# A mixture-of-experts layer in which the last slots are 11 tiles of two chunks and 7 of one chunk, in place of 18 tiles of two

## The reference

```
x = x + attention(layernorm(x))                       # 8 x 512 x 256, causal
xn = layernorm(x, gamma, beta)
probs = softmax(xn @ gate_w);  w, idx = top_k(probs, 2);  w = w / sum(w)
h = gelu(xn @ w1[e] + b1[e])                          # 256 -> 1024, exact gelu
out = sum over the two experts of w_e * (h @ w2[e] + b2[e])   # 1024 -> 256
x = x + (xn + out)
```

## Time and profile before

| | |
|---|---|
| time, median of 3 runs | 1096.27 us |
| the profiled execution | 1091.03 us |
| its span, first to last instruction | 1089.1 us |
| TensorE busy | 911.5 us (84%) |
| VectorE busy | 731.8 us (67%) |
| ScalarE busy | 596.7 us (55%) |
| GpSimd busy | 471.4 us (43%) |
| mean granted TensorE clock | 0.887 of full |

### The profile page before, as it was taken

The page is one execution under the profiler, slowest core; times in us unless marked ns, Lnnn a source line. Parts: engine busy times, 40 slices in busy tenths (PEclk is TensorE's granted clock), DMA queues, the critical chain, the costliest instruction groups (busy, mean ns, idle before and its releaser), DMA issues.

```text
span 1089.1 us, 21658 instructions
## 1 busy us (share of the span) xinstructions
PE 911.5 (84%) x7052; PEld 598.0 (55%) x7052; DVE 731.8 (67%) x1632; ACT 596.7 (55%) x1085; POOL 471.4 (43%) x536
## 2 busy tenths in 40 slices
PE   4788868775878787888887898879988999999995
PEld 2444423222242323333332787768877898989894
DVE  6353688775648798887883686766756676767663
ACT  2554537563747677766766564444634454545451
POOL 2000003323424565646565557454564555455542
PEclk9898988887678887879785999989999999999998
DMA  9887757764665757575735552232322333332322
GB/s 208 266 287 247 257 191 221 227 160 112 187 205 153 212 158 201 144 212 137 196 86 164 180 114 41 42 84 41 46 42 46 55 46 55 46 55 45 56 45 25
DMA packets 150568, 144.22 MB, mean 132 GB/s; under 512 B 42112, under 2 KB 128896, under 8 KB 150336
## 3 DMA queue, kind: packets, MB, share of 16 engines
q1 hardware_dynamic: 117856, 97.92, 31.4%
q0 software_dynamic: 17024, 20.81, 11.9%
q10 hardware_dynamic: 15584, 24.12, 6.9%
HBM read 88.44 MB, written 54.10 MB: 131 GB/s over the span
## 4 chain that ended last, share of the span: by engine, by line
PE 38%; DMA 17%; issue 11%; DVE 10%; SPq 7%; POOL 7%; ACT 6%; DVEq 2%; ACTq 0%; POOLq 0%
PE banks L729 13%; PE banks L713 13%; DMA qk_parts<-weights 4%; DMA arena<-in_L_ffn_w 4%; SPq L1779 3%; POOL slot_tokens L1556 3%; PE banks L635 2%; PE banks L592 2%; PE banks L647 2%; POOL out L1600 2%; DMA weighed_values<-arena 1%; DVE arena L1160 1%; DMA late_weights<-arena 1%; SPq L1766 1%; PE banks L577 1%
## 5 line engine op out<-in xcount | busy, mean ns | idle before, releaser
L935 ACT ACTIVATE arena<-banks,arena 128x256 f32<-128x256 f32 x312 | 158.9, 561 | 197.9 <-issue 130.3
L729 PE MATMUL banks<-weights,arena 128*128 x1872 | 217.0, 275 | 9.0 <-DVE arena L1419 8.9
L713 PE MATMUL banks<-arena,weights 128*128 128x256 f16 x1872 | 213.1, 274 | 3.9 <-DMA weights<-late_weights 3.0
L1600 POOL DMA_INDIRECT out<-arena x78 | 128.0, 1641 | 202.5 <-DVE arena L1430 101.2
L729 PEld LDWEIGHTS banks<-weights,arena 128*128 128x128 f16 x1872 | 183.8, 99 | 34.6 <-issue 12.1
L713 PEld LDWEIGHTS banks<-arena,weights 128*128 x1872 | 183.7, 98 | 27.2 <-issue 4.9
L592 PE MATMUL banks<-arena 50*128 50x128 f16 (+3 forms) x512 | 125.7, 352 | 36.2 <-ACT arena L862 13.9
L564 PE MATMUL banks<-arena 48*128 48x128 f16 (+3 forms) x512 | 103.2, 345 | 34.8 <-DVE arena L1158 25.9
L1419 DVE SCALAR_TENSOR_TENSOR arena<-arena 128x512 f16<-128x512 f32 x156 | 119.3, 765 | 5.6
L592 PEld LDWEIGHTS banks<-arena 50*128 50x128 f16 x512 | 38.2, 102 | 147.1 <-issue 52.7
L1417 DVE TENSOR_SCALAR arena<-arena 128x512 f16<-128x512 f32 x156 | 78.2, 501 | 58.4 <-ACT arena L935 56.9
(11 more groups left out here) (172 smaller groups left out, 1373.7 us busy)
## 6 DMA issues: line engine op xcount, KB each, us to landing
weights<-in_L_ffn_w ACTq DMA_DIRECT2D x16, 1024.0 KB, 9.1
arena<-in_L_ffn_w SPq DMA_DIRECT2D x32, 512.0 KB, 5.3
qk_parts<-weights SPq DMA_DIRECT2D x96, 128.0 KB
arena<-qk_parts SPq DMA_DIRECT2D x128, 96.0 KB, 3.4
v_rows<-weights SPq DMA_DIRECT2D x8, 1024.0 KB, 9.6
weighed_values<-arena SPq DMA_DIRECT2D x32, 256.0 KB
token_rows<-arena SPq DMA_DIRECT2D x12, 512.0 KB, 5.5
weights<-in_L_attn_x ACTq DMA_DIRECT2D x8, 512.0 KB, 8.9
```

The costliest lines, as they stand in the source:

```text
L713: m = pe.matmul(bank[:, c * TILE:(c + 1) * TILE], w1[:, k, wp, f:f + P], xp[:, k, :], start=(i == 0), stop=(i == len(terms) - 1))
L729: m = pe.matmul(bank[:, c * D:(c + 1) * D], hp[:, f, c * P:(c + 1) * P], w2[:, f // (FC // 2), wp, f % (FC // 2), :], start=(f == 0 and i ...
L935: m = act.activation(h_32[r % 2][:, c, :], banks[:, 1 + c2, c * TILE:(c + 1) * TILE], ACT.Gelu, bias=b1_now[j % 2][:, 2 * c2 + c:2 * c2 + ...
L1600: g.indirect_dma_start(acc_dram[:, :], bass.IndirectOffsetOnAxis(slot_of(j, c), 0), y[j % 2][:, c, :], None, compute_op=ALU.add).then_inc( ...
```

## The change

The last 18 tiles of two chunks become two parts: 11 tiles of two chunks, then 7 tiles of one chunk. There are still 39 tiles, but 71 chunks in place of 78. Part 3 takes an expert's pairs of chunks and the first expert's tile count takes up what the 7 single ones can't hold; part 4 takes the odd chunks, one tile each. In a tile of one chunk every operation of the round works on half: gather and scatter once, 2 turns in place of 4, the 48 products of `hidden` with 128 moving columns in place of 256, 24 products of `expert_out` in place of 48 with 256 columns as before, gelu and split on half the columns, `make_y` and `weigh_b2` once. Part 4 adds a layout: `lay_out` without a table load, and `lay_slots` with 9 copies in place of 8 (the ninth writes spare rows behind the last tile; part 3 gets it too). In all parts four step numbers are inserted into `lay_out`, which only part 3 fills, and `lay_slots` starts 8 ticks later (10 in the first part). Waits on the gather's and scatter's semaphores count chunks.

```
+    FULL = full
+    REST = (N * TOPK - FULL * TILE + E * (P - 1)) // P
+    SINGLES = E - 1
+    PAIRS = -((SINGLES - REST) // TC)
+    PARTS += [(B, PAIRS, FULL, TC), (B, SINGLES, FULL + PAIRS, 1)]
+    TILES = FULL + PAIRS + SINGLES
...
-            base = max(ranked_at[batches - 1] + 16, 7 * NG * UNIT + 88)
-            for step in range(12):
+            base = max(ranked_at[batches - 1] + 16, 7 * NG * UNIT + 88) + (168 if i > ALL else 0)
+            for step in range(16):
                 at(base + 3 * step, "lay_out", (i, step))
-            at(base + (8 if i == 0 else 56), "table", i)
-            for e_ in range(E):
-                at(base + (44 if i == 0 else 72) + 4 * e_, "lay_slots", (i, e_))
+            if i <= ALL:
+                at(base + (8 if i == 0 else 56), "table", i)
+            for e_ in range(E + 1):
+                at(base + (54 if i == 0 else 80) + 4 * e_, "lay_slots", (i, e_))
...
-                    m = pe.matmul(bank[:, c * TILE:(c + 1) * TILE], w1[:, k, wp, f:f + P], xp[:, k, :],
+                    m = pe.matmul(bank[:, c * TILE:c * TILE + WIDTH[j]], w1[:, k, wp, f:f + P],
+                                  xp[:, k, 0:WIDTH[j]],
...
-                for c in range(TC):
+                for c in range(CHUNKS[j]):
                     for f in (2 * pair, 2 * pair + 1):
...
-                    m = act.activation(h_32[r % 2][:, c, :], banks[:, 1 + c2, c * TILE:(c + 1) * TILE], ACT.Gelu,
+                    m = act.activation(h_32[r % 2][:, c, 0:WIDTH[j]],
+                                       banks[:, 1 + c2, c * TILE:c * TILE + WIDTH[j]], ACT.Gelu, ...
...
+                elif step in (5, 6, 7, 8):
+                    if i != ALL:
+                        return
+                    if step == 5:
+                        m = own.mark(v.scalar_tensor_tensor(odd, tiles_e, -float(TC), chunks_int, ALU.mult, ALU.add))
+                    elif step == 6:
+                        m = own.mark(v.tensor_reduce(odd[:, 0:1], odd, AX.X, ALU.add))
+                    elif step == 7:
+                        m = own.mark(v.tensor_scalar(odd[:, 0:1], odd[:, 0:1], -float(SINGLES), 0.0, ALU.add, ALU.max))
+                    else:
+                        m = own.mark(v.tensor_tensor(tiles_e[:, 0:1], tiles_e[:, 0:1], odd[:, 0:1], ALU.add))
...
+                if e_ == E and i < ALL:
+                    return
...
+                if e_ == E:
+                    v.tensor_copy(slot_token[i][:, bass.ds(to, LOCAL)], spare_row).then_inc(sem("laid_out"), 1)
+                    return
...
-                    w.wait_ge(sem("added"), 32 * (j - 1))
-                for c in range(TC):
+                    w.wait_ge(sem("added"), 16 * CHUNKS_TO[j - 1])
+                for c in range(CHUNKS[j]):
```

More of the change, by code:

```diff
@@ L472, in side_made, with gathered_in @@
             return side[(stage, n)][1]
+        def gathered_in(j):
+            return sem(f"gathered{j % 3}"), 16 * sum(CHUNKS[j % 3:j + 1:3])
         def exp_use(u, i):
```

119 lines of the change are left out of this document (66 added, 53 removed).

## The result

| | before | after |
|---|---|---|
| time, median of 4 runs | 1096.73 us (1094.32 to 1097.45) | 1066.96 us (1062.55 to 1068.28) |
| the profiled execution | 1091.03 us | 1062.55 us |
| its span | 1089.1 us | 1060.8 us |
| TensorE busy | 911.5 us (84%) | 888.3 us (84%) |
| VectorE busy | 731.8 us (67%) | 718.0 us (68%) |

The ratio of after to before is 0.9725, with a 95% interval of 0.9693 to 0.9758: the change is faster, by 29.8 us on the medians and by 28.5 us between the two profiled executions. The forecast was 28.5 us less. (The median before has one run more than the one ahead of the change.) I compare the starts of `hidden` (L713 before, L730 after) tile by tile, since each ends one round and begins the next. A single round is the round of a tile of one chunk; the table's round is the one in which the lists of the last parts land.

What follows compares the result with a forecast made beforehand. TensorE was taken to bound the full rounds, VectorE's chain the new single ones. 32.8 us gained over the last seven rounds less 4.3 for layouts gave 28.5: 1091.0 to 1062.5 profiled, 1068 on the median, range 1056 to 1083.

Steps and rivals of the forecast that it cites:

- `hidden`, the step that was mis-sized: TensorE's 48 products of `hidden` in a single round: 36 + 31 = 67 ns each, 3.2 us in all.
- the chain of the forecast: Single round: gelu, splits, then VectorE's bias copy and turn_low set the next `hidden`, 6.55 to 6.95 us after the last.
- the register load for the bias: VectorE, behind the fourth split: register load takes 0.75 to 1.11 us from its second half's start, 0.48 covered.
- the stated 6 to 7.7: Single round, forecast 6.8 us: the main step is wrong if one takes under 6 or over 7.7 us.
- Gelu and split: ScalarE and VectorE on half the columns: gelu pair 0.84 us, split halves 0.365 and 0.48, with a large fixed share.
- Rival 1: Single rounds: gelu and split fall nearly to half, register loads stay covered; round 5.5 us, total 1059; chance 0.10.
- The end: After the last `hidden`: its products end 4.1 us sooner, one make_y less saves 0.4, one scatter less 3.91.
- The layouts: Copies of `lay_slots`: part 3 gains 1.6 us, part 4 loses 3.3, the first part loses 2.6; together 4.3 lost.
- 2, the stationary operand bounds `hidden`: Single rounds: 48 loads cost as before, a group stays at 1.31 us, round 8.9, total 1083; chance 0.14.
- 3, nine uncovered copies: Part 4's layout: nine copies at 1.58 us uncovered, 14.2 us in place of 3.3, total 1079; chance 0.09.
- 4, a falling clock: Single rounds: waits drop TensorE mostly to 1.2 GHz, round 11.7 us, total 1102, slower; chance 0.04.
- 5: Single tiles wait for something full-size not seen; the change saves nothing to speak of, within 3 us; chance 0.03.

Runs made afterwards that it cites:

- e1: Kernel after, with the 7 single tiles reading one fixed expert's weights at a fixed address in both products, register load kept: 1055.16 us.
- e6: Kernel after, with part 3's slot copies 8 ticks earlier, at tick 72 as before the change: 1088.65 us (kernel before on that chip 1120.70).
- e7: Kernel after, with the copies of parts 3 and 4 every 14 ticks, not 4, and part 4's layout 112 ticks later: 1078.23 us (before there 1120.70).
- e8: Kernel after, with the first part's copies 8 ticks earlier (46 in place of 54): 1086.26 us (kernel before on that chip 1120.70).
- e9: Kernel after, unedited, timed again against the kernel before on a third chip: 1068.97 us, ratio 0.9788 (0.9712 to 0.9864).
- e10: Kernel after, with each gather 20 ticks earlier, ahead of the scatter: 1063.24 us (kernel before on that chip 1093.22).
- e3: Kernel after, with TensorE's register load of the expert's number ahead of the tile's turn, no longer in `hidden`: 1069.83 us.
- e2: e1, with TensorE's register load of the expert's number also left out for the single tiles: 1069.11 us.
- e4: Kernel after, with `hidden` on all 256 columns in the single tiles: 1087.06 us.
- e5: Kernel after, with gelu and split at full size in the single tiles, products still halved: 1096.72 us (kernel before on that chip 1120.70).
- e11: Kernel after with the edits of e7, e3 and e10, and the bias copy 16 ticks earlier: 1053.29 us, ratio to before 0.9651.
- e12: e11 plus the edit of e8: 1049.10 us, ratio to before 0.9591 (0.9529 to 0.9653).

## Why the prediction was right, and where only its sum was

**`hidden`, the step that was mis-sized.** The forecast took 36 ns for load and product and 31 for the register operations. The second term is exact (87 - 56). The first is 56: products of 8 columns don't tell the pace at 128. So `hidden` took 4.2 us and not 3.2. It moved the bound too, so this part of the mechanism was wrong: the forecast had VectorE's chain set the next H, at 6.55 to 6.95; with 56 + 31 ns TensorE's own work is 4.19 + 0.23 + 2.74 = 7.16 and its wait 0.2 to 0.5, and that is the round. With the mis-sized term smaller, as in e1, the chain of the forecast stands: fourth split ends at H + 5.26, next H at 6.13, under the forecast's 5.63 and 6.55, mostly since the groups come at 0.87 (three from 1028.44, the first split's second half, to 1031.05) and not 0.94, and the register load for the bias leaves 0.26 us of wait, at the low end of the 0.27 to 0.63 that the forecast had. The 7.44 us lie within the stated 6 to 7.7; only the second round, 7.81 with its wait for the gather, lies above.

The Trainium skill (TensorE: Matmul & The Clock Gate, "Back-to-back issue gap") gave 81 ns a product; measured are 56 at a fixed address and 87 with the register operations. Read as the cost of this round it is nearer than my 67, but it has no term for what the difference consists of.

**Gelu and split.** 0.81 and 0.36 + 0.485 us, forecast 0.84, 0.365 and 0.48: a large fixed share and the rest by columns is right. From the two sizes of each (561 and 456 ns, 501 and 358, 765 and 485) the fixed share comes out as 351 ns for gelu and 215 and 205 for the halves of the split, where the forecast had 230 for the split's first half. Rival 1, which had them fall nearly to half, is dead by these rows.

**The end.** From the last H to the last product 7.2 us in place of 6.5 (again `hidden`), one scatter and one make_y less. From the last H to the end of the span it is 15.4 us in place of 23.9, 8.4 less as forecast: the 0.7 us lost on `hidden` came back for the most part behind the last scatter, whose tail is 7.4 us in place of 8.0. That is luck.

**The layouts.** Part 3 gained 1.9 (1.6 forecast), part 4 lost 3.0 (3.3), the first part lengthened TensorE's wait for the mask by 2.6 (2.6). e6, e7 and e8 show each to be due to the copies, though their sizes differ between profiles: TensorE's wait for the mask scatters by 3 us (e8), and part 4's layout costs 1.1 us more where the granted clock falls behind the gap, which the forecast doesn't have. What the forecast lacked is how little reaches the end: of the 2.6 us 1.6 were left at the first `hidden`, and the rounds between it and the table's took 1.7 us less in this pair of profiles. Such rounds also differ between profiles of one program (the one ahead of the table's took 15.9 us in the profile after and 13.1 in e9), so it isn't shown that the change did that. The exact agreement of the total is in this sense luck: -3.5 and +3.3. So is part of its place in the scatter of the measurement, as e9 shows with 24.3 us.

**The rivals.** 2, the stationary operand bounds `hidden`: not at 1.31 us a group, but in its kind it was nearest. The pace of loads with their register operations is the bound, at 1.03 to 1.05. 3, nine uncovered copies: 3.0 us and not 14.2. 4, a falling clock: 1.00 in the six single rounds and up to the last product; from 1057 to 1060 us, with no product left, the granted clock was 0.60. Full rounds behind a layout's gap did run at a lower clock in other profiles (last section), single ones didn't. 5: no.

## What to carry to other kernels

When the columns of a product are halved, the load of the stationary operand and the operations that make its address stay; add them as they stand in the queue of the engine, and take the pace of the product from a run of nearly the same size, not from a much smaller one. An operation of VectorE or ScalarE has a fixed share, so half the work took 0.63 to 0.81 of the time here. A small operation with a register load in front cost nothing here when a third of a round lay between one and the next (e7). Bunched in two rounds, nine of them cost 3.0 us, and on a path without cover seven took 1.16 us each: spread them before you count them. And a wait that an edit takes away can move work together elsewhere: e10's early gathers gained only where the copies were spread too.

## What the runs showed of the hardware

- A stationary load with its product of 128 columns: 56 ns at fixed addresses (48 in 2.68 us), 87 ns with two register operations of 46 ns for three loads. Where the queue had work ahead of it, it was less: 78 ns in e3 (3.76 us for 48), and in the first single tile 67 (3.22 us). That the register operations had run ahead there, while a full tile's products were worked off, is my reading and wasn't tried by itself.
- A register load on TensorE, which shows as a wait of 0.2 to 0.5 us before `hidden` when the loads take their address from it, cost nothing when they didn't, whether issued (e1) or not (e2).
- In e1 a wait of 2.3 us of TensorE in part 4's layout was followed by a `hidden` in 6.91 us in place of 5.42, and the next round took 12.49 us; a wait of the same length in the kernel after was followed by 5.42 us. So it is in other profiles: part 4's second round took 12.2 to 12.6 us at a granted clock of 0.86 to 0.89 in e1, e2, e3 and e8, and 11.3 to 11.4 at 1.00 in the kernel after, e4, e5 and e9, with gaps of 2.3 to 2.5 us ahead of it in all of them. What decides between the two is open. Part of that stretch of e1 ran at the lower clock, 1.2 GHz: the granted clock is 0.78 there, and 1.00 in the kernel after. Two rows of e1's timeline, its window, and the window of the kernel after:

```profile
866.07 1.70 PE L749 MATMUL banks<-weights,arena 128*128 x12 [2.30 <-DVE arena L1466]
867.57 6.91 PE L732 MATMUL banks<-arena,weights 128*128 128x256 f16 x48
```

```profile
868.00:874.00 6.00, 6.00 (x45) 4.81 (x44) 3.19 (x9) 2.60 (x6) 1.55 (x1) 0.78 0.00 0
```

```profile
869.40:874.60 5.20, 5.20 (x50) 4.60 (x49) 1.85 (x7) 2.04 (x4) 0.19 (x1) 1.00 0.00 0
```

- The round ahead of the table's took 13.1 to 19.3 us in the eleven profiles with the gathers in their old place (before, after and nine of the runs), and 10.93 in e10, e11 and e12, the three with early gathers. In the kernel after and in e9 TensorE's turn waits for a gather in it (e10). On the chip of e5 to e8 the round took 18.3 to 19.3 us, and `hidden` has waits of up to 1.06 us between products there that the profile ascribes to nothing ("issue"). Why is open; no run with early gathers was made on that chip.
